# Query products of a gated cross-attention block: two half-width channel blocks per bank, or one full-width block

## The reference, cut to what matters

```
xn  = layernorm(x)
Q   = xn @ W_q.T ; K = ctx @ W_k.T ; V = ctx @ W_v.T        # ctx: 120 rows per batch
s   = Q K^T / sqrt(32) - slope(head) * (query_pos - key_pos) ; masked
a   = exp(s - max) / (1 + sum(exp(s - max)))
x   = x + tanh(g_xattn) * (a V) @ W_o.T
xn2 = layernorm(x)
xr  = mu_r * xn2 + (1 - mu_r) * previous_token(xn2) ; xk likewise with mu_k
out = x + tanh(g_ffn) * sigmoid(xr @ W_r.T) * (relu(xk @ W_k.T)^2 @ W_v.T)
```

## Time and profile before

| | |
|---|---|
| median of 3 runs | 1359.54 us |
| the profiled execution: its time | 1362.47 us |
| the profiled execution: its span | 1360.7 us |
| mean granted TensorE clock | 0.995 |
| PE busy | 1321.2 us (97% of the span) |
| PEld busy | 1117.5 us (82%) |
| DVE busy | 1078.5 us (79%) |
| ACT busy | 863.8 us (63%) |
| POOL busy | 730.2 us (54%) |

### The profile page before, as it was taken

How to read it: one execution, slowest core, us unless ns; L and a number is a source line. 1 busy time by engine, 2 the same in 40 slices (tenths; PEclk the granted TensorE clock), 3 DMA queues, 4 the chain that set the end, 5 groups by cost and what they waited for, 6 DMA issues and landing times. The chain is left out here.

```text
span 1360.7 us, 32788 instructions
## 1 busy us (share of the span) xinstructions
PE 1321.2 (97%) x10864; PEld 1117.5 (82%) x10864; DVE 1078.5 (79%) x2889; ACT 863.8 (63%) x2928; POOL 730.2 (54%) x766
## 2 busy tenths in 40 slices
PE   7989899999999999999999999999999999999988
PEld 6887788878888887888888887878888888888867
DVE  5437879798887979798887978888797979889764
ACT  5227485775848586675848586675848577575842
POOL 0103564655656565655656565565656466565641
PEclk9999999999999999999999999999999999999999
DMA  7822102020200202020110302020110202010000
GB/s 263 240 76 66 32 2 78 10 63 24 58 28 13 73 1 63 24 63 24 47 39 0 85 1 63 24 63 24 35 50 1 85 1 63 24 63 23 17 17 31
DMA packets 53074, 66.48 MB, mean 49 GB/s; under 512 B 23024, under 2 KB 29168, under 8 KB 52976
## 3 DMA queue, kind: packets, MB, share of 16 engines
q1 hardware_dynamic: 52976, 65.52, 16.2%
HBM read 40.87 MB, written 24.64 MB: 48 GB/s over the span
## 5 line engine op out<-in xcount | busy, mean ns | idle before, releaser
L796 ACT ACTIVATE probs<-probs,neg_max 128x120 f32<-128x120 f32 x1024 | 390.4, 388 | 27.3 <-DVE neg_max L1064 27.3
L1355 POOL TENSOR_TENSOR probs<-probs,recip 128x960 f32<-128x960 f32 x128 | 229.2, 1791 | 209.3 <-DVE recip L1075 209.3
L1060 DVE SCALAR_TENSOR_TENSOR probs<-mask_in,score_bank 128x120 f32<-128x120 f32 x1024 | 213.8, 271 | 123.1 <-PE score_bank L461 95.3
L402 PE MATMUL rotating<-xnt_or_act,w_query 128*128 128x256 f32 x1536 | 197.3, 285 | 5.3 <-DVE xnt_or_act L1046 5.3
L402 PE MATMUL rotating<-w_gate,mixed_gate 128*128 128x512 f32 x768 | 194.9, 403 | 6.7 <-DVE xs L1086 3.8
L796 ACT ACTIVATION_READ_ACCUMULATOR probs<-probs,neg_max 128x1 f32 x1024 | 197.7, 193 | 0.0
L402 PEld LDWEIGHTS rotating<-xnt_or_act,w_query 128*128 128x128 f32 x1536 | 188.7, 191 | 10.0 <-ACT query_t L788 7.9
L402 PE MATMUL rotating<-w_proj,attn_t 128*128 128x512 f32 x768 | 194.2, 402 | 1.5 <-DVE xnt_or_act L1046 1.5
L402 PE MATMUL rotating<-w_value,xnt_or_act 128*128 128x512 f32 x720 | 178.2, 396 | 0.0
L402 PE MATMUL rotating<-mixed_key,w_key 128*128 128x512 f32 x720 | 174.5, 394 | 0.0
L1064 DVE TENSOR_REDUCE neg_max<-probs 128x4 f32<-128x480 f32 x256 | 167.2, 653 | 8.8
(11 more groups left out here) (129 smaller groups left out, 2255.2 us busy)
## 6 DMA issues: line engine op xcount, KB each, us to landing
xs<-in_x_dram SPq DMA_DIRECT2D x64, 256.0 KB, 2.8
out_dram<-gated SPq DMA_DIRECT2D x64, 256.0 KB, 3.0
value_scratch<-gated SPq DMA_DIRECT2D x16, 240.0 KB, 2.6
mask_in<-in_mask_dram SPq DMA_DIRECT2D x16, 240.0 KB, 2.7
keys_t<-key_scratch SPq DMA_DIRECT2D x16, 240.0 KB, 3.5
values<-value_scratch SPq DMA_DIRECT2D x16, 240.0 KB, 3.8
probs<-in_ctx_t_dram SPq DMA_DIRECT2D x6, 480.0 KB, 7.1
key_scratch<-query_t SPq DMA_DIRECT2D x12, 240.0 KB, 4.9
```

Source lines behind the costliest of these rows:

```text
L402: mm = pe.matmul(bank, stationary(a, c), moving(b, c), start=(i == 0), stop=(i == MATMULS - 1))
L796: e = act.activation(probs[:, t % 2, head, :], probs[:, t % 2, head, :], ACT.Exp, bias=neg_max[:, t % 2, head:head + 1], accum_out=sums[:, ...
L1060: z = dve.scalar_tensor_tensor(out=probs[:, t % 2, head, :], in0=neg_dist[:, t, :], scalar=SLOPES[head], in1=score_banks[j][:, g * NK:(g + ...
L1355: pool.tensor_tensor(part, part, recip[:, t % 2, heads].unsqueeze(2).to_broadcast((P, H // 2, NK)), ALU.mult)\
```

## The change

Each query step makes all 512 tokens of one channel block, with 12 matmuls of 512 columns. So each step needs all four tiles of the first norm. On PE, `turn2(2)` and `turn1(3)` now stand ahead of the first query step. `scores` of tile 0 waits for the four evictions, one for each of its groups g; the scores of tile 2 need no query wait of their own. In the last batch, where no query is made, `turn2(2)` comes ahead of the first gate product of the tail instead of behind it. The same holds for the query products ahead of the loop: their first now waits for four tiles instead of two. The orders of ACT, DVE, POOL and SP are as they were; ACT's `query_out` reads the same 128x512 bank.

```diff
             def scores(b, t, g):
-                if t % 2 == 0 and g % 2 == 0:
-                    pe.wait_ge(read["query"], b * 4 + t + g // 2 + 1)
+                if t == 0:
+                    pe.wait_ge(read["query"], b * CT + g + 1)
...
-            def query(b, u, steps):
-                half, pair = divmod(u, 2)
-                pe.wait_ge(read["turn1"], b * QT + (half + 1) * QT // 2)
-                for n in range(2 * steps[0], 2 * steps[-1] + 2):
-                    i, step = divmod(n, MATMULS)
-                    m = pair * 2 + i
-                    mm = product(bank_of["query", u][:, i * S // 2:(i + 1) * S // 2],
-                                 lambda s, c: w_query[:, s, c, m * P:(m + 1) * P],
-                                 lambda s, c: xnt_or_act[:, s, c, half * S // 2:(half + 1) * S // 2], [step])
-                return mm
+            def query(b, m, steps):
+                if m == 0 and steps[0] == 0:
+                    pe.wait_ge(read["turn1"], (b + 1) * QT)
+                return product(bank_of["query", m][:], lambda s, c: w_query[:, s, c, m * P:(m + 1) * P],
+                               lambda s, c: xnt_or_act[:, s, c, :], steps)
...
                 use("proj", 3)
-                use("query", 0)
+                use("turn2", 2)
+                use("turn1", 3)
                 if last:
                     pe.wait_ge(read["value"], b * QT)
                     gate(b, 0, range(MATMULS), tail_bank).then_inc(done["gate"], 1)
-                use("turn2", 2)
-                use("query", 1, range(9))
-                use("turn1", 3)
-                use("query", 1, range(9, MATMULS))
+                use("query", 0)
+                use("query", 1)
                 use("turn2", 3)
                 use("query", 2)
                 use("query", 3)
...
-            def query_out(b, u):
-                half, pair = divmod(u, 2)
-                act.wait_ge(done["query"], b * 4 + u + 1)
-                act.mul(query_t[:, pair * 2:pair * 2 + 2, half * S // 2:(half + 1) * S // 2],
-                        bank_of["query", u][:].rearrange("p (m q) -> p m q", m=2), SCALE).then_inc(read["query"], 1)
+            def query_out(b, m):
+                act.wait_ge(done["query"], b * CT + m + 1)
+                act.mul(query_t[:, m, :], bank_of["query", m][:], SCALE).then_inc(read["query"], 1)
```

## The result

The changed kernel takes 1484.53 us in the median of 4 runs (1481.71 to 1487.95), against 1359.86 us for the kernel before (1358.67 to 1360.37, 4 runs): a ratio of 1.0919, 95% interval 1.089 to 1.0949. The profiled execution took 1487.95 us with a span of 1486.2 us, 125.5 us longer than the span before. Its mean granted clock is 0.959, where it was 0.995.

The account below looks back on a forecast made before the run. The prediction took PE, busy 97% of the span, as the bound. It summed 5.5 + 2.4 + 0.2 + 0.1 + 0.4 = 8.6 us a batch, 129 us in 15 batches, on 1359.5: 1488 us, range 1465 to 1508.

Parts of the forecast that it names:

- the wait for the probabilities: PE's wait in turn_probs for POOL, after the scores: about 0.4 us a batch, between nothing and 1.0.
- way to the first query step, from the residual's start: DVE's residual at 622.40 to PE's first query product at 629.53, plus 0.2 us for tile 3's turn at low clock.
- turn and last two steps: PE, behind query step 1: one turn of 0.35 us, then 24 matmuls of 512 columns in 5.58 us.
- scores: Last group of tile 0's scores waits for ACT's eviction of query step 3: 0.1 us, between nothing and 0.7.
- The gap: PE between projection and first query step: 7.4 us without a product, only two turns of 0.35 us in it.
- The clock: Granted clock halves behind PE's idle time in every batch: 2.4 us in query products, 0.2 us in tile 3's turn.
- What is queued behind the later turn: Work after turn2(3) on ACT, POOL and DVE: bias 1.9 us behind the scores, 0.6 us later, less 0.24 us slack.
- The first rival: Granted clock holds in all or most batches: 6.0 us a batch, 90 us, 1450 us; chance 0.10.
- the second: Rival: norms ready in time, shorter query work between projection and scores gains 1.25 us a batch, 1341 us; chance 0.02.
- the fourth: Rival: matmuls of 512 columns no cheaper than twice 256, adding 0.65 us a batch, 1498 us; chance 0.05.
- the third: Rival: clock loss 3.3 us, turn 0.35, scores 0.3, probabilities' wait 1.0; 10.5 us a batch, 1517 us; chance 0.08.
- The first four products, ahead of the loop: Query products before the loop: gain 0.65 us and wait for two more tiles, under 1 us, left out.

Follow-up runs that it names:

- the order alone: The kernel before, with half-width query steps kept, and only the turns on PE placed where the changed kernel has them: 1458.73 us, ratio 1.0722.
- the shorter chain: The changed kernel with tile 3's first-norm statistics, reciprocal deviation and normalisation moved earlier on DVE and POOL, nothing left out: 1491.97 us, ratio 1.0972.
- the filled gap: The changed kernel with 24 matmuls of 512 columns per batch, results thrown away, added in PE's idle time before the first query step: 1450.2 us, ratio 1.0672.
- the early turn: The changed kernel with turn2(3) right behind turn1(3) on PE, and its copy and mix_gate_high(1) ahead of the query evictions on ACT: 1469.24 us, ratio 1.08.

## Why the prediction was right, point by point

The forecast was 1488 us, and 1484.53 was measured. The signs it named in PE's timeline are there: the waits of 1.5, 3.05 and 1.4 us (the last just under the 1.5 to 2 us named), the wait for the probabilities, a first query step of about 4.7 us and a turn of the loop of 85.3 us, inside the 83 to 88 named. The terms, each by its measurement in the batch shown:

| term, us a batch | forecast | measured |
|---|---|---|
| way to the first query step, from the residual's start | 7.13 + 0.2 for the turn at the low clock | 7.56 |
| first two query steps, beyond 5.58 at the full clock | 2.4 | 1.81 |
| turn and last two steps | 0.35 + 5.58 | 0.35 + 5.65 |
| scores | 0.1 | 0.08 |
| wait for the probabilities | 0.4 | 0.42 |

- **The gap** was read from DVE's rows, and DVE ran them again at the same distances up to the norm of tile 3. The experiment with the order alone shows that it is the order that opens it; those with the shorter chain, that its end is DVE's last low part and not the norm.
- **The clock** fell in each of the 15 batches. The 2.4 us for the products, taken from the one such gap of the tail, was too much: the timeline shows 1.8 to 2.1 us for the first two steps in 14 batches and 2.3 in one. The turn of tile 3, on the other hand, ran at the low clock in the batch shown (1.12 us where the earlier trace rows have 0.60), and from it to the first query step it was 0.46 us more than in the filled gap, above my 0.2. Together they come to 2.3 us by the filled gap, against my 2.6. The rule of the Trainium skill that the prediction cited points the same way as the tail's rows, from which the 2.4 us were taken. It held in all 15 batches. Ahead of the loop, where only transposes stood between the products for 5.0 us, the clock fell in two runs of six.
- **What is queued behind the later turn** was right in size, partly by luck, and the early turn shows its cause. The bias came 783.74 - 782.06 = 1.68 us behind the scores, not 1.9, so 0.4 us later than before and not 0.6. But the 0.24 us that I took off as slack were none: with PE waiting, the turn starts 0.24 us behind POOL's end all the same (790.00 + 1.79 = 791.79 on POOL, 792.03 on PE). The two errors cancel.
- **The first rival** is refuted by the granted clock of 0.959, the second by the three waits, the fourth by 5.65 and 11.10 us for wide runs. Of the third, only the turn's part came true.
- **One step failed**: "The first four products, ahead of the loop, gain their 0.65 us and wait for two more tiles: under 1 us, left out." In the kernel before and in the changed kernel PE's timeline has there

```profile
83.54 11.78 PE L402 MATMUL rotating<-xnt_or_act,w_query 128*128 128x256 f32 x96 [0.54 <-DVE xnt_or_act L1046]
```

```profile
84.96 12.81 PE L402 MATMUL rotating<-xnt_or_act,w_query 128*128 128x512 f32 x48 [1.74 <-DVE xnt_or_act L1036]
97.70 1.25 PE L461 MATMUL score_bank<-keys_t,query_t 32*128 32x120 f32 x32
```

  The wait grew by 1.2 us, and the products took 97.70 - 84.96 = 12.74 us where the narrow ones took 11.71 (the scores began at 95.25): 2.2 us more in all. The clock fell here too, which the step had left out:

```profile
84.00:85.00 1.00, 0.04 (x1) 1.00 0.00 0
...
86.00:87.00 1.00, 1.00 (x4) 0.50 0.00 0
```

  In the run with the shorter chain the same wait was followed by products at the full clock:

```profile
83.94 11.19 PE L402 MATMUL rotating<-xnt_or_act,w_query 128*128 128x512 f32 x48 [1.74 <-DVE xnt_or_act L1036]
```

  They took 11.12 us (the scores began at 95.06), so the added wait less the gain was 0.6 us, under 1 us as the step says. What failed is only the clock's 1.6 us, once in the run.

## What to carry to other kernels

Before an operand is widened, ask when its last column is ready, and what work covers the time until then: here 0.7 us of matmul time was bought with the two half-width steps that had covered 5 us of another engine's chain. Price a new gap on TensorE twice, once for itself and once for the products behind it, if they run at the lower clock: here 2.3 us on top of a gap of 7.9 us, and 1.7 us on top of one of about 6.8. These are averages; in two of the runs it differed by over 1 us from batch to batch, so one batch is not enough to read it from. And when a chain is to be shortened, list everything that the engine does up to the last thing PE waits for, as a wait that moves one place on gives nothing back.

## What the runs showed of the hardware that I had not expected

- The same gap can end with the clock at either level. Ahead of the loop, six runs (the changed kernel and all experiments with wide products) do the same work and wait 1.73 or 1.74 us before the first products, with only transposes in the microseconds before. The granted clock fell there in two of them, the changed kernel and the early turn, and stayed at 1.00 in the other four. In the gaps of the loop of the changed kernel it fell 15 times in 15.
- What a fall costs differs too. In the order-alone run, 48 narrow matmuls took 7.0 to 7.3 us or 8.0 to 8.1 us behind gaps that differ by less than 0.2 us. What decides between them is open.
- A DVE operation took over twice as long beside POOL. Four parts of `mix_gate` (two inputs from SBUF) took 1.14 us at 768.51 in the changed kernel, with POOL idle, and 2.98 us at 630.66 in the kernel before, with POOL at its own two-input subtractions:

```profile
768.51 1.14 DVE L1116 SCALAR_TENSOR_TENSOR diff<-diff,mu,xn2t 128x128 f32<-128x128 f32 x4
```

```profile
630.66 2.98 DVE L1126 SCALAR_TENSOR_TENSOR diff<-diff,mu,xn2t 128x128 f32<-128x128 f32 x4
```

  That POOL is the cause wasn't tried by itself. The Trainium skill, "SBUF — State Buffer", section "Who interferes with whom", states that VectorE and GpSimd share a pair of ports, and that a VectorE instruction with two SBUF inputs contends with a GpSimd instruction that reads SBUF; the two rows agree. The mix that cost 1.92 us instead of 1.11 in the run with the shorter chain also lay beside such a subtraction (764.00 to 765.04 on POOL).
